# Differential attention with a feed-forward branch: the order of score pieces, two value blocks in the first unit, another order of the first loads, and two output blocks added on VectorE

## The reference, cut to what matters

```python
xn  = layernorm(x)                                   # x: [1, 1024, 256] f32
qkv = xn @ Wqkv                                      # Wqkv: [256, 768]
q1, k1, q2, k2, v = split(qkv, [128, 256, 384, 512]) # q, k: 16 heads of 8; v: 16 heads of 16
lam = exp(lq1 @ lk1) - exp(lq2 @ lk2) + LAMBDA_INIT
A1  = causal_softmax(q1 @ k1.T / sqrt(8)) @ v        # "branch 0" in the kernel
A2  = causal_softmax(q2 @ k2.T / sqrt(8)) @ v        # "branch 1"
d   = A1 - lam * A2
attn = (1 - LAMBDA_INIT) * d / rms(d) @ Wproj
ffn  = fp8(gelu(fp8(xn) @ fp8(Wg[0])) * (fp8(xn) @ fp8(Wg[1]))) @ fp8(Wl)
out  = x + attn + ffn                                # [1, 1024, 256]
```

## Time and profile before

| what | us |
|---|---|
| median of three runs | 193.35 |
| the profiled execution, its own time | 192.92 |
| its span, first to last instruction | 191.1 |
| TensorE busy | 182.0 (95%) |
| ScalarE busy | 168.1 (88%) |
| VectorE busy | 93.6 (49%) |
| GpSimd busy | 59.4 (31%) |

### The profile page before, as it was taken

The page is one execution under the profiler, slowest core; times in us unless marked ns, Lnnn a source line. Parts: engine busy times, 40 slices in busy tenths (PEclk is TensorE's granted clock), DMA queues, the critical chain, the costliest instruction groups (busy, mean ns, idle before and its releaser), DMA issues.

```text
span 191.1 us, 3572 instructions
## 1 busy us (share of the span) xinstructions
PE 182.0 (95%) x1452; PEld 78.1 (41%) x1452; DVE 93.6 (49%) x220; ACT 168.1 (88%) x146; POOL 59.4 (31%) x71
## 2 busy tenths in 40 slices
PE   6799999799999999999989999999999999999992
PEld 6685344464333323233324334333423434433481
DVE  0975799322223140550274012704750999579852
ACT  2476967999999999999999999999999999999820
POOL 8517600051116321450343053307301630532000
PEclk9999999999999999999999999999999999999999
DMA  5969377780000000000088794000000000000033
GB/s 172 406 254 269 87 193 203 202 193 15 0 0 3 0 0 3 0 0 3 13 199 197 192 194 95 0 0 3 0 0 3 0 3 0 0 0 3 0 113 113
DMA packets 8148, 14.97 MB, mean 78 GB/s; under 512 B 1984, under 2 KB 5312, under 8 KB 8128
## 3 DMA queue, kind: packets, MB, share of 16 engines
q1 hardware_dynamic: 7440, 14.05, 27.3%
q10 hardware_dynamic: 688, 0.66, 1.0%
HBM read 5.26 MB, written 1.05 MB: 33 GB/s over the span
## 4 chain that ended last, share of the span: by engine, by line
PE 58%; ACT 35%; DMA 3%; SPq 1%; DVE 1%; issue 0%
ACT probs L454 35%; PE ps L990 19%; PE ps L978 12%; PE ps L824 9%; PE ps L893 7%; PE ps L830 4%; PE ps L1020 3%; DMA w_q<-L_attn_Wqkv 3%; PE ps L931 1%; PE ps L838 1%; PE ps L814 1%; PE ps L1025 1%; SPq L241 0%; DVE area L581 0%; ACT probs L442 0%
## 5 line engine op out<-in xcount | busy, mean ns | idle before, releaser
L454 ACT ACTIVATE probs<-ps,shift 128x1536 f32<-128x1536 f32 x96 | 141.2, 1540 | 1.6 <-PE ps L978 1.0
L990 PE MATMUL ps<-probs,v_all 128*32 128x512 f32 (+3 forms) x768 | 78.3, 496 | 0.5 <-DVE o_t L654 0.4
L363 POOL TENSOR_SCALAR_AFFINE_SELECT probs<-probs 128x1024 f32<-128x1024 f32 (+1 forms) x40 | 36.7, 917 | 103.9 <-ACT probs L454 103.8
L978 PE MATMUL ps<-q_st,k_st 32*128 32x512 f32 (+3 forms) x384 | 49.9, 420 | 0.4 <-ACT probs L454 0.4
L978 PEld LDWEIGHTS ps<-q_st,k_st 32*128 32x128 f32 x384 | 22.5, 182 | 57.8 <-ACT probs L454 29.9
L654 DVE STREAM_TRANSPOSE o_t<-ps 128x512 f32<-128x512 f32 x16 | 11.5, 717 | 45.4 <-PE ps L990 45.4
L990 PEld LDWEIGHTS ps<-probs,v_all 128*32 128x32 f32 x768 | 16.2, 108 | 19.0 <-issue 13.2
L824 PE MATMUL ps<-xn_t,w_q 128*128 128x256 f32 (+1 forms) x46 | 17.5, 491 | 0.8 <-DMA w_q<-L_attn_Wqkv 0.8
L893 PE MATMUL ps<-area 128*128 128x512 fp8e4 x64 | 14.5, 379 | 0.0
L442 ACT ACTIVATE probs<-ps 128x512 bf16<-128x512 f32 x16 | 9.2, 597 | 3.5 <-PE ps L893 3.0
L581 DVE TENSOR_TENSOR area<-ps,probs 128x512 fp8e4<-128x512 f32 x16 | 10.7, 690 | 1.0 <-ACT probs L442 0.7
(11 more groups left out here) (81 smaller groups left out, 125.2 us busy)
## 6 DMA issues: line engine op xcount, KB each, us to landing
q_st<-parts SPq DMA_DIRECT2D x32, 128.0 KB, 2.8
k_st<-parts SPq DMA_DIRECT2D x32, 128.0 KB, 2.8
probs<-L_ffn_w_gating SPq DMA_DIRECT2D x4, 512.0 KB, 7.8
probs<-L_ffn_w_linear SPq DMA_DIRECT2D x1, 1024.0 KB, 12.0
w_q<-L_attn_Wqkv SPq DMA_DIRECT2D x2, 384.0 KB, 5.8
out<-probs SPq DMA_DIRECT2D x3, 256.0 KB, 2.2
x_sb<-L_attn_x SPq DMA_DIRECT2D x2, 256.0 KB, 4.0
x_sb<-L_attn_x ACTq DMA_DIRECT2D x2, 256.0 KB, 4.3
```

The source lines that it names most:

```text
L363: pool.affine_select(out=blocks, in_=blocks, pattern=pattern, compare_op=ALU.is_ge, fill=0.0, base=0, channel_multiplier=-1).then_inc(mask ...
L454: act.activation(probs[:, at:at + PER_UNIT, :].rearrange("p s u -> p (s u)"), ps[:, 3 * (n % 2):3 * (n % 2) + 3, :].rearrange("p b n -> p ...
L978: ins = pe.matmul(ps[:, bank, at:at + wide * P], k_st[rows, g % STACKS, kb * P:(kb + 1) * P], q_st[rows, g % STACKS, queries], start=True, ...
L990: ins = pe.matmul(ps[32 * j:32 * j + 32, 6, q0 % HALF:q0 % HALF + wide * P], v_all[:, g % HG, kb, 32 * j:32 * j + 32], probs[:, slot + j, ...
```

## The change

Scores: within a unit the wide pieces are issued first (chunks 1 and 5, 384 columns before 128). Value blocks 2 and 3 both go into unit 0, through bank 6 and with a wait on the 15th `hidden_ready` instead of the 16th; the last two feed-forward steps swap their bank pairs for it, and `scores(1)` waits for the 16th instead. The second branch's queries and keys begin at unit 5 and end at 33 (8 and 37 before), its norms are at 19, 27, 35, 37 (23, 31, 39, 41). Loads: x's blocks 0 to 3 go singly, even ones on SP and odd ones on ScalarE's queue, blocks 4 to 7 on ScalarE's queue; `Wqkv` is cut by columns, q1 and k1 (256 KB) first. At the end blocks 2 and 3 are added by VectorE, with no identity product.

```diff
-PAIR = [2, 3, 0, 1, 2, 3, 0, 1, 2, 0, 1, 3, 0, 1, 2, 3]
+PAIR = [2, 3, 0, 1, 2, 3, 0, 1, 3, 0, 1, 2, 0, 1, 3, 2]
+V_BANK = (6, 6, 7, 6)
-Y_BANK = (7, 7, 0, 1, 2, 2, 3, 4)
+Y_BANK = (7, 7, 0, 0, 2, 2, 3, 4)
-V_AT = {0: (2,), 1: (3,), 2: (4,), 3: (5,), 4: (6,), 5: (7,)}
-QK_AT = {8: (4, 0, 0, 256), 9: (4, 0, 256, 256), 13: (4, 1, 0, 512), 17: (5, 0, 0, 512), 20: (5, 1, 0, 256),
-         21: (5, 1, 256, 256), 25: (6, 0, 0, 512), 29: (6, 1, 0, 512), 32: (7, 0, 0, 256), 33: (7, 0, 256, 256),
-         37: (7, 1, 0, 512)}
-NORM_AT = {23: 0, 31: 1, 39: 2, 41: 3}
+V_AT = {0: (2, 3), 1: (4,), 2: (5,), 3: (6,), 4: (7,)}
+QK_AT = {5: (4, 0, 0, 512), 8: (4, 1, 0, 256), 9: (4, 1, 256, 256), 13: (5, 0, 0, 512), 17: (5, 1, 0, 512),
+         20: (6, 0, 0, 256), 21: (6, 0, 256, 256), 25: (6, 1, 0, 512), 29: (7, 0, 0, 512), 32: (7, 1, 0, 256),
+         33: (7, 1, 256, 256)}
+NORM_AT = {19: 0, 27: 1, 35: 2, 37: 3}
+def wide_first(c):
+    return sorted(range(len(CHUNKS[c])), key=lambda p: -CHUNKS[c][p][1])
...
 # SP
-            for b in (0, 4):
-                sp.dma_start(x_sb[:, b:b + 2, :], x_rows[:, b:b + 2, :]).then_inc(x_in[b // 2], 16)
-            for k in range(KC):
-                sp.dma_start(w_q[:, k, :], w_qkv[k * P:(k + 1) * P, :]).then_inc(wq_in, 16)
+            for b in (0, 2):
+                sp.dma_start(x_sb[:, b, :], x_rows[:, b, :]).then_inc(x_in[b // 2], 16)
+            w_rows = w_qkv.rearrange("(k p) n -> p k n", p=P)
+            sp.dma_start(w_q[:, :, 0:C], w_rows[:, :, 0:C]).then_inc(wq_in, 16)
+            sp.dma_start(w_q[:, :, C:3 * C], w_rows[:, :, C:3 * C]).then_inc(wv_in, 16)
...
 # GpSimd: the fourth square follows mask(2, 5), not mask(3, 2)
 # ScalarE
-            for b in (2, 6):
+            for b in (1, 3):
+                act.dma_start(x_sb[:, b, :], x_rows[:, b, :]).then_inc(x_in[b // 2], 16)
+            for b in (4, 6):
                 act.dma_start(x_sb[:, b:b + 2, :], x_rows[:, b:b + 2, :]).then_inc(x_in[b // 2], 16)
...
 # VectorE: split 5 and norm round 0 before keep(1, 0); keep(1, 1) after norm round 1, keep(2, 1) after branch 1's bounds
+            for b in (2, 4):
+                dve.wait_ge(y_ready, b // 2 + 1)
+                dve.tensor_tensor(y[:, b:b + 2, :] ..., ps[:, Y_BANK[b], :], x_sb[:, b:b + 2, :] ..., ALU.add)
...
 # TensorE, scores
-                for p in range(2):
+                for turn in range(2):
                     for c, j, bank in items:
+                        p = wide_first(c)[turn]
...
 # TensorE, the end
-                pe.wait_ge(res_ready, TB // 2)
-                for b in (2, 3):
-                    project(b, 0, start=True)
-                    residual(b)
-                    project(b, 1).then_inc(y_ready, 1)
+                project(2, 0, start=True)
+                project(3, 0)
+                project(2, 1)
+                project(3, 1).then_inc(y_ready, 1)
```

More of the change, by code:

```diff
@@ L208, in diff_attention_ffn_kernel @@
         x_in = [sem(f"x_in{b}") for b in range(TB // 2)]
-        wq_in, wg_in, wl_in, wp_in, lam_in_s = (sem(n) for n in (
-            "wq_in", "wg_in", "wl_in", "wp_in", "lam_in_s"))
+        wq_in, wv_in, wg_in, wl_in, wp_in, lam_in_s = (sem(n) for n in (
+            "wq_in", "wv_in", "wg_in", "wl_in", "wp_in", "lam_in_s"))
         ident_set, causal_set, v_ones, ones_set, picks_set = (sem(n) for n in (
@@ L304, in _ @@
                     maxima(g)
-            for b in (0, 2):
-                sp.wait_ge(y_copied, b + 2)
+            sp.wait_ge(y_copied, 2)
+            sp.dma_start(out_rows[:, 0:2, :], y[:, 0:2, :]).then_inc(y_out, 16)
+            for b in (2, 4):
+                sp.wait_ge(y_added, b // 2)
                 sp.dma_start(out_rows[:, b:b + 2, :], y[:, b:b + 2, :]).then_inc(y_out, 16)
-            sp.wait_ge(y_added, 1)
-            sp.dma_start(out_rows[:, 4:6, :], y[:, 4:6, :]).then_inc(y_out, 16)
-            sp.wait_ge(y_added, 2)
+            sp.wait_ge(y_added, 3)
             sp.dma_start(out_rows[:, 7, :], y[:, 7, :]).then_inc(y_out, 16)
@@ L373, in _ @@
                     mask(g, c)
-                    if (g, c) in ((1, 2), (1, 5), (2, 5), (3, 2)):
-                        square_of(4 + ((1, 2), (1, 5), (2, 5), (3, 2)).index((g, c)))
+                    if (g, c) in ((1, 2), (1, 5), (2, 5)):
+                        square_of(4 + ((1, 2), (1, 5), (2, 5)).index((g, c)))
+                    if (g, c) == (2, 5):
+                        square_of(7)
                     if (g, c) in ((4, 4), (5, 2), (6, 2), (7, 0)):
@@ L466, in _ @@
             act.activation(newton[:, 1, 112:113], newton[:, 0, 0:1], ACT.Sqrt)
-            for b in (0, 1, 2):
+            for b in (0, 1):
                 whole(b)
@@ L470, in _ @@
             act.activation(newton[:, 3, 112:128], newton[:, 0, 112:128], ACT.Sqrt).then_inc(rms_ready, 1)
-            for b in (3, 6):
-                whole(b)
-            act.wait_ge(y_copied, 5)
+            whole(6)
+            act.wait_ge(y_copied, 3)
             act.dma_start(out_rows[:, 6, :], y[:, 6, :]).then_inc(y_out, 16)
@@ L731, in _ @@
             keep(0, 1)
-            keep(1, 0)
             split(5)
             norm_round(0)
-            keep(1, 1)
+            keep(1, 0)
             split(6)
             norm_round(1)
+            keep(1, 1)
             keep(2, 0)
@@ L740, in _ @@
             norm_round(2)
-            keep(2, 1)
             norm_round(3)
@@ L749, in _ @@
             bound1.bias()
+            keep(2, 1)
             keep(3, 0)
@@ L797, in _ @@
             dve.wait_ge(res_ready, TB // 2)
[L798 to L801, removed]
+            for b in (2, 4):
+                dve.wait_ge(y_ready, b // 2 + 1)
+                dve.tensor_tensor(y[:, b:b + 2, :].rearrange("p b c -> p (b c)"), ps[:, Y_BANK[b], :],
+                                  x_sb[:, b:b + 2, :].rearrange("p b c -> p (b c)"), ALU.add).then_inc(y_added, 1)
+            dve.wait_ge(y_ready, 5)
             dve.tensor_tensor(y[:, 7, :], ps[:, Y_BANK[7], 0:C], x_sb[:, 7, :], ALU.add).then_inc(y_added, 1)
@@ L852, in _ @@
             transposes(0)
-            pe.wait_ge(wq_in, 32)
+            pe.wait_ge(wq_in, 16)
             for i in range(2):
@@ L864, in _ @@
             transposes(2)
+            pe.wait_ge(wv_in, 16)
             project_values(0, 6)
@@ L900, in beside @@
                     if n == 0:
-                        pe.wait_ge(hidden_ready, len(FFN))
+                        pe.wait_ge(hidden_ready, 15)
                     if b >= 6:
                         pe.wait_ge(v_out, 4)
-                    project_values(b, 7 - (b // 2 + 1) % 2)
+                    project_values(b, V_BANK[b // 2])
                 if n in QK_AT:
@@ L907, in beside @@
                     if n == min(QK_AT):
-                        pe.wait_ge(v_out, TB)
+                        pe.wait_ge(v_out, 6)
                     elif (k, at) == (0, 0):
@@ L966, in scores @@
                 if n == 1:
-                    pe.wait_ge(hidden_ready, 15)
+                    pe.wait_ge(hidden_ready, 16)
                 if n >= 2:
@@ L970, in scores @@
                 items = [((PER_UNIT * u + e) // J, (PER_UNIT * u + e) % J, 3 * (n % 2) + e) for e in range(PER_UNIT)]
-                for p in range(2):
+                for turn in range(2):
                     for c, j, bank in items:
-                        if p == len(CHUNKS[c]):
+                        if turn == len(CHUNKS[c]):
                             continue
+                        p = wide_first(c)[turn]
                         kb, wide, q0 = CHUNKS[c][p]
@@ L1000, in values @@
                 (kb, wide, q0), *more = CHUNKS[c]
-                if g == 0 and c < 2:
-                    pe.wait_ge(v_out, (6, TB)[c])
+                if g == 0 and c == 0:
+                    pe.wait_ge(v_out, TB)
                 if c == 0 and g > 0:
@@ L1074, in ending @@
                 project(6, 0, start=True)
+                pe.wait_ge(res_ready, TB // 2)
                 residual(6)
```

8 lines of the change are left out of this document (4 added, 4 removed).

## The result

The changed kernel takes **190.53 us** (median; 190.44 to 190.88) against 193.34 for the kernel before (193.13 to 193.37): a ratio of 0.986 (95% interval 0.9843 to 0.9878). The forecast was 191.0. The profiled execution took 190.61, its span is 188.8 against 191.1. Almost right in sum, the forecast is wrong in one of its three parts.

A forecast was written before the change was run, and what follows sets the result against it. TensorE and ScalarE were taken to hold the end in turn. Loads 0.3, loop 1.4 and end 0.65 sum to 2.35: 192.92 becomes 190.57, or 191.0 as median with 0.43 added; range 190.0 to 192.3.

The forecast's parts named there:

- Loads: Before the loop: x's first blocks landing sooner gain 0.3 us, bounds a loss of 0.3 and a gain of 0.7.
- what is late next: Before the loop: blocks 6 and 7, last on ScalarE's queue, land by 9.7; priced at 0, may cost 0.2 us.
- the bound of 0.7: Before the loop: most the loads can win, as 256 KB at 374 GB/s take 0.70 us.
- No longer ends last: Before the loop: the weight part needed first is 256 KB instead of 768, so its wait no longer ends last.
- The starving rival: Blocks 6 and 7 starve on ScalarE's queue behind SP's; kernel slower, 193.8 us if they land at 14; chance 0.05.
- Value blocks and tables: In the loop: 0.54 us earlier up to unit 40, 0.15 past it from the norm gone at unit 41.
- Wide pieces first: In the loop: 0.05 us a unit in 32 units, 1.6 at most; 0.7 up to unit 40, 0.7 after.
- order is worth nothing: Rival, in the loop: the weight load is exposed wherever the short piece stands; total gain 1.3, 192.05 us; chance 0.15.
- The end: After the loop: TensorE's last eight products start sooner with four instructions gone; gain 0.65 us, bounds 0.15 and 0.87.

## Why the prediction was right, and where it was not

**Loads: wrong.** The step that failed is "what is late next ... I price it at 0", for the loads behind the first pair: with it the loads brought -0.43 in place of +0.3. Blocks 0 and 1 gained even more than the bound of 0.7, and then the wait moved to pairs 2 and 3. Three things in that step differ from the trace. The landing of pair 3 was estimated at 9.7 with 374 GB/s; in fact it was 10.65, since the rate fell to 171 and 216. Pair 2 was not asked about at all, and it is the one whose lateness reached TensorE first, as VectorE takes a pair's statistics before it finishes the pair ahead. And the way from pair 3's landing to its copied turn, put at 3.8, took 15.61 - 10.65 = 4.96, and as much in the two kernels with the old order of pieces and with Wqkv by rows; so a landing costs time from about 15.03 - 4.96 = 10.1 on, and not from 11.2. "No longer ends last" was wrong for the weights too, by 0.14 (8.02 against 7.88).

The starving rival held half: right in its place, wrong in its mechanism. SP's large rows explain part of pair 3; pair 2 is late without them. What the runs show is a condition: only kernels with four single blocks at the head and both late pairs on ScalarE's queue had pair 2's statistics after 7.8: the changed kernel 8.26, the same loads with the old order of pieces 8.67 and with the norm at 41 8.98, Wqkv by rows 9.50, the weights held back 7.81. Taking away either half of the condition mends pair 2 (7.08 and 7.15). Each of these is one profiled execution. Why both queues are supplied slowly under it stays open.

**Value blocks and tables: size off.** The forecast split the loop at unit 40. Up to there its two halves were -0.16 for the tables (0.54 less the 0.7 of the pieces) and 0.7 for the pieces; measured +0.10 (old order of pieces, against before) and 0.67 (before with wide pieces). The second closes, the first came out 0.26 better. Past it, 0.15 was given to the tables, and they brought 0.72: exponentials 40 to 48 take 11.86 before, 11.76 with the pieces alone, 11.38 with the tables alone, and 11.39 in the changed kernel, which is 8 x 1.424, the floor. So 0.48 lie in the eight units from 40 on, where the norm of unit 41 and its wait are gone; the other 0.24 come after exponential 48, and no run takes them apart. A likely reading is that the pieces of the feed-forward in units 44 and 45 now find TensorE ahead, so that the norm cost not only what it pushed itself but also the lead it took from what follows. That is argued, not shown: no run isolates the norm.

**Wide pieces first: right**, 0.05 a unit and 1.08 in the changed kernel against 1.4 in the sum (0.7 and 0.7). By itself it would be 1.42. One number beside it does not add up: the rival "order is worth nothing" keeps 0.3 to 0.35 in the loop, but by the sum's own terms -0.16 and 0.15 are left, about nothing, which gives 192.4 and not 192.05.

**The end: right.** 0.58 up to the last addition, 0.64 for the span with the end alone. In the changed kernel the part after the last addition is also shorter, by 0.2 (3.06 in place of 3.28), of which the single change shows half (3.18).

That the sum was near is luck in good part: -0.73 at the beginning and +0.63 in the rest, most of it in the loop, offset each other. For the profiled execution the sum gave 190.57, and it took 190.61. The forecast of 191.0 added 0.43, by which the profiled execution of the kernel before lay under its median; the changed kernel's lies 0.08 above its own, and so the median came out 0.47 under the forecast.

## What to carry to other kernels

When a load is pulled forward, write down when every later load must be there and ask for each which wait takes the place, the second as well as the last; then test the order of the loads alone, since it is cheap and the rate need not be what the old order showed (171 GB/s here in place of 378). A wait on a full engine may cost more than itself, by the lead that would hide the next overfull units (here argued, not isolated). Where a short and a long piece follow each other on one row group, put the long one first, so that the short one's weights load behind it (0.44 in place of 0.48 a unit here).

## What the runs showed of the hardware that was not expected

**A longer wait of TensorE went with a fall of its clock.** In the kernel with the norm back at unit 41, TensorE stood 1.67 after a stretch in which it had been nearly full, and some 10 us at 1.2 GHz followed; after 0.64 in the kernel before, and 0.92 at unit 42 in the changed one, the granted clock stayed at 1.00. One profiled execution shows it, so that the wait is the cause isn't shown. The spread of that kernel goes with the clock: the mean granted clock of its executions is 0.97 to 0.98 in the four from 194.1 to 197.1, 0.99 at 193.4 and 194.0, and 0.998 or more in the five from 191.0 to 192.1. Where in those executions the clock fell is not known.

**The moment at which TensorE reaches its full rate at the start differs.** The 14 products before the first transposes are the same in all kernels, but they end at 6.53 in the kernel before and at 7.87 with x as before and Wqkv by columns:
```profile
1.58 6.29 PE L831 MATMUL ps<-ident 128*128 128x128 f32 x28 [1.58 <-POOL ident L327]
7.71 0.60 PE L826 MATMUL ps<-ident,probs 128*128 128x128 f32 x4
```
One instruction of them takes 0.21 and later 0.11 from start to start, a factor of 2 as between the levels of 1.2 and 2.4 GHz, and the change between the two falls at 4.4 to 7.7 us in different kernels. That it is the clock is inferred from the factor: the column of the granted clock reads 1.00 in both stretches. In the kernel with x as before the first transposes start 0.74 late, behind these products, though x was there, the first product with weights 0.63 late (9.08), and the first exponential as much (36.51).

With x's first blocks sooner these 14 products are what the first transposes wait for in other kernels too: block 0 is normalized by 6.04 with the norm at 41 and by 6.82 with blocks 2 and 3 as one pair, and the transposes start at 7.39 and 7.09. No run has fewer of them, so what that would bring is open. A difference of some tenths at the beginning has to be read from the landings, not from the end time.
